# One 512 KB output store split into four pieces of 128 KB, issued over three steps of the schedule

## The reference, cut to what matters

```python
xn = _layernorm(x, axis=-1)
# attention: 16 heads of 64, rotary q and k, a distance bias kb per head
scores = jnp.einsum('bhqd,bhkd->bhqk', q, k) * SCALE
attn = jax.nn.softmax(scores + kb[None], axis=-1)
out = jnp.einsum('bhqk,bhkd->bhqd', attn, v)      # -> (8, 512, 1024) @ out_w.T -> (8, 512, 256)
# experts: 16, top 1, at most 256 tokens each; relu(x w1) w2, times the gate
x = x + attention(xn) + experts(xn)
```

## Time and profile before

| | |
|---|---|
| median of three runs | 1230.52 us |
| the profiled execution's own time | 1232.55 us |
| its span, first to last instruction | 1230.8 us |
| mean granted TensorE clock | 0.944 |
| TensorE busy | 1086.2 us (88%) |
| VectorE busy | 1014.4 us (82%) |
| ScalarE busy | 999.5 us (81%) |
| GpSimd busy | 817.6 us (66%) |
| stores of line 1183 | 7, first issued at 481.6 us, last at 1136.3 us |

### The profile page before, as it was taken

One profiled execution on the slowest core, in us unless ns is written; L12 is line 12 of the kernel. 1 busy time (PEld: TensorE's weight loads), 2 busy tenths in 40 slices (PEclk: granted clock), 3 DMA queues, 4 the chain that ended last, 5 costly groups with the idle time before them and its releaser, 6 DMA issues.

```text
span 1230.8 us, 35480 instructions
## 1 busy us (share of the span) xinstructions
PE 1086.2 (88%) x14436; PEld 797.2 (65%) x14436; DVE 1014.4 (82%) x2061; ACT 999.5 (81%) x1986; POOL 817.6 (66%) x481
## 2 busy tenths in 40 slices
PE   4840699999789999999999999999999998999874
PEld 4830588989556666666666666666666666666653
DVE  7883799999578888888898788888988887888872
ACT  2694688886279898899889899889889898988991
POOL 3135100000399988888899789888998898898741
PEclk8565799999899999999999999999999999999996
DMA  8716566773136565766665666575557657756673
GB/s 252 296 40 213 180 221 224 255 243 134 35 61 126 117 102 116 148 104 93 143 129 94 123 130 109 100 143 117 105 113 148 97 109 131 129 95 114 106 123 69
DMA packets 390289, 165.79 MB, mean 135 GB/s; under 512 B 340722, under 2 KB 380671, under 8 KB 390128
## 3 DMA queue, kind: packets, MB, share of 16 engines
q1 hardware_dynamic: 377856, 143.26, 54.4%
q0 software_dynamic: 4352, 12.41, 2.9%
q10 hardware_dynamic: 7920, 7.87, 2.1%
HBM read 58.79 MB, written 21.00 MB: 65 GB/s over the span
## 4 chain that ended last, share of the span: by engine, by line
PE 38%; DMA 13%; ACT 10%; POOL 7%; issue 4%; SPq 2%; DVE 1%; POOLq 0%; ACTq 0%
DMA pt_dma<-prob_parts 9%; PE ps_s L1377 8%; PE ps_x L1333 8%; PE ps_o L1410 7%; PE ps_t L1390 6%; ACT prob L1130 6%; PE ps_x L1352 5%; PE ps_x L1343 4%; DMA ot<-ctx_parts 4%; POOL prob_parts L1005 3%; ACT pt_pe L1114 2%; POOL ctx_parts L1013 2%; SPq L949 1%; POOL parts L999 1%; ACT val_hi L1093 1%
## 5 line engine op out<-in xcount | busy, mean ns | idle before, releaser
L1130 ACT ACTIVATE prob<-prob,neg_max 128x512 f32<-128x512 f32 x512 | 364.0, 714 | 4.7 <-DVE neg_max L1251 2.6
L1251 DVE CUSTOM_DVE_ANT_0 prob<-ps_s,strips,score_scale 128x512 f32<-128x512 f32 x512 | 360.1, 745 | 7.5 <-PE ps_s L1377 5.7
L1005 POOL TENSOR_TENSOR prob_parts<-prob,prob_parts 128x1024 f16<-128x1024 f32 x128 | 273.6, 2138 | 55.4 <-ACT prob_parts L1120 55.1
L1377 PE MATMUL ps_s<-parts 32*128 32x512 f16 x3072 | 189.1, 376 | 1.1 <-DVE parts L1297 1.0
L1257 DVE SCALAR_TENSOR_TENSOR pt_pe<-ps_t,pt_pe 128x1024 f16<-128x1024 f32 x128 | 155.8, 1217 | 36.0 <-ACT pt_pe L1114 36.0
L1390 PEld LDWEIGHTS ps_t<-ident,prob 128*128 128x128 f32 x1024 | 109.7, 141 | 57.3 <-issue 39.0
L995 POOL TENSOR_TENSOR rot<-prods 128x1024 f32<-128x1024 f32 x61 | 144.3, 2366 | 2.7 <-DVE prods L1217 2.7
L1333 PE MATMUL ps_x<-xcur,wqkv_hi 128*128 128x512 f16 x480 | 143.3, 380 | 2.7 <-DVE pt_dma L1217 1.3
L1390 PE MATMUL ps_t<-ident,prob 128*128 128x128 f32 x1024 | 139.8, 279 | 3.0 <-DVE pt_pe L1257 3.0
L1120 ACT CAST prob_parts<-prob 128x1024 f16<-128x1024 f32 x128 | 133.6, 1044 | 2.1
L1114 ACT ACTIVATE pt_pe<-ps_t 128x1024 f16<-128x1024 f32 x128 | 130.7, 1021 | 3.4 <-PE ps_t L1390 3.3
(11 more groups left out here) (207 smaller groups left out, 2639.5 us busy)
## 6 DMA issues: line engine op xcount, KB each, us to landing
raw<-in_L_ffn_w_dram SPq DMA_DIRECT2D x32, 1024.0 KB, 5.2
xa<-in_L_attn_x_dram SPq DMA_DIRECT2D x8, 512.0 KB, 6.6
xt_dram<-xth SPq DMA_DIRECT2D x8, 512.0 KB, 5.1
slots_dram<-zeros SPq DMA_DIRECT2D x4, 1024.0 KB, 8.2
xa<-slots_dram SPq DMA_DIRECT2D x16, 256.0 KB, 5.3
expert_dram<-xa POOLq DMA_DIRECT2D x16, 256.0 KB, 6.7
xcur<-xt_dram SPq DMA_DIRECT2D x8, 512.0 KB, 4.5
res<-in_L_attn_x_dram ACTq DMA_DIRECT2D x8, 512.0 KB, 4.0
```

The lines of the kernel that those rows point to most:

```text
L1005: nc.gpsimd.tensor_tensor(prob_parts[:, n % 2, 1], prob[:, (2 * n + 1) % 3], prob_parts[:, n % 2, 0], ALU.subtract).then_inc(prob_lo, 1)
L1130: nc.scalar.activation(prob[:, s % 3, q, :], prob[:, s % 3, q, :], ACT.Exp, bias=neg_max[:, 2 * (s % 3) + q:2 * (s % 3) + q + 1], scale=-1 ...
L1251: nc.vector.tensor_tensor_reduce(prob[:, s % 3, q, :], ps_s[u][:], strips[:, HG * j + u, start:start + S], score_scale[:, 0:1], 3.0e38, AL ...
L1377: last = nc.tensor.matmul(ps_s[h][:], parts[rows, 2 * F % 5, a, f, t * P:(t + 1) * P], parts[rows, (2 * F + 1) % 5, c, f, :], start=(i == ...
```

## The change

The one store of 512 KB becomes four of 128 KB, one for each of the four blocks of 128 rows: the first behind quad 4, the second behind quad 5, the third and fourth together behind quad 6. Each adds 16 to `y_stored`, so the two waits on it count 64 a batch.

```diff
-            sp.wait_ge(y_stored, 16 * NB)
+            sp.wait_ge(y_stored, 64 * (NB - 1) + 16)
...
-                if q == 4 and b:
+                if 4 <= q <= 6 and b:
                     act.wait_ge(x_free, fills_before(b, 8))
-                    act.dma_start(out[b - 1].rearrange("(t p) m -> p t m", p=P), yacc[:]).then_inc(y_stored, 16)
+                    for t in ((0,), (1,), (2, 3))[q - 4]:
+                        act.dma_start(out[b - 1, t * P:(t + 1) * P, :], yacc[:, t, :]).then_inc(y_stored, 16)
...
-                    wait(dve, y_stored, 16 * b)
+                    wait(dve, y_stored, 64 * b)
```

## The result

The changed kernel takes 1247.23 us (median of 6 runs, 1239.94 to 1251.41); the kernel before, beside it, 1230.77 us (6 runs, 1230.05 to 1232.17). The ratio is 1.0128, with a 95% interval of 1.0098 to 1.0159: 1.0 to 1.6% slower, 16.5 us by the medians. The forecast was 1235.2 us, 4.7 us slower, and the range ended at 1239.5. The direction and the place were right and the size was not. The runs of the changed kernel also spread over 11.5 us, those of the kernel before over 2.

What follows compares the result with a forecast made beforehand. No single engine is full and the order of waits decides, with TensorE the bound around the change. Terms 0 + 0 + 3.2 + 1.5 = 4.7 us slower gave 1235.2 us, range 1229.8 to 1239.5.

Steps and rivals of the forecast that it cites:

- Removed: 0: End of quad 4: taking away seven 512 KB stores frees no waiting engine, 0 us; bound on a gain 3.5 us.
- The rival on the faster side: End of quad 4: the old store holds back the probability transposes, the pieces do not; 3.5 us faster, 1227.0 us; chance 0.08.
- Added to ScalarE: 0: Behind quads 5 and 6: three more issues a batch at about 0.39 us are covered by casts, 0 us.
- That rival: End of quad 6: ScalarE is held by the two issues, up to 5.5 us on top, about 1240 us; chance 0.08.
- VectorE's wait: 3.2 us: Quad 7: `read_y` waits for the last piece, delaying TensorE's fill y1 past its slack by 3.2 us in all.
- I take 1.9 + 0.6 = 2.5 after its issue, T6 + 2.9: Behind quad 6: last piece lands after the smallest DMA's 1.9 us plus 0.6 us of data, in every batch.
- T6: In each batch, the start of the cast that ends quad 6; the forecast counts issue, landing and `read_y` from it.
- the far end, T6 + 4.6: Behind quad 6: the last piece lands like the longest 512 KB store, 4.2 us; 13.4 us slower, 1244 us; chance 1 in 20.
- The slack of 0.6 us: Quad 7: `read_y` ends before y1 starts, behind 1.40 us of value products, so 0.6 us of delay is covered.
- The further 1.1 us that I gave batch 4: Quad 7, batch 4: TensorE already waits there for a transpose DMA, so 1.1 us more of delay is covered.
- Traffic: 1.5 us: Behind quad 6: pieces take DMA time from the transpose TensorE needs; 0.5 us each in batches 1, 4 and 6.
- Rival C: In the probe: a queue's packets wait for a copy in flight on the other, so pieces land in about 4.5 us.

Runs made afterwards that it cites:

- The change without its hold: The changed kernel with plain copies for transposes, but its two pieces behind quad 6 read a constant table and VectorE does not wait for them; 1219.7 us, ratio 0.9874.
- the base: The kernel before with its transposing DMAs replaced by plain copies of the same 512 KB in 256-byte packets; 1220.4 us, ratio 0.9874 to the kernel before.
- the probe: A separate kernel with only two queues, ScalarE's storing pieces and SyncE's loading or copying beside them; two pieces alone land in 2.30 to 2.34 us.
- the change with copies: The changed kernel with its transposing DMAs replaced by plain copies of the same 512 KB in 256-byte packets; 1246.3 us, ratio 1.0071 to the kernel before.

## Why the prediction was wrong

**Removed: 0.** Right as far as the runs resolve. The change without its hold has three of the four pieces out of the gap and takes the base's time, 1219.7 for 1220.4 us, so taking the store out of its gap frees nothing. The rival on the faster side falls.

**Added to ScalarE: 0.** Right, 0.84 us for both issues, and 0.96 us to the next instruction. That rival falls too.

**VectorE's wait: 3.2 us.** Right in its mechanism, wrong in its size. The step that failed is "I take 1.9 + 0.6 = 2.5 after its issue, T6 + 2.9" for all batches. It holds where no load is ahead of the pieces and the transpose is over early: batch 7 T6 + 2.5, batch 2 T6 + 2.9, and the probe has 2.3 us from the first issue. It fails a little in batches 1 and 6, T6 + 3.4 and 3.6, where the transpose moves until T6 + 2.1 and 2.3, and most where the `xcur` load is ahead: T6 + 4.3 to 5.5. Set against the same seven starts of the kernel before, `read_y` is later by 0.8, 1.0, 4.2, 3.2, 2.8, 0.8 and 1.3 us, 14.0 in all, where my holds sum to 6.8. Of these TensorE waits 9.3 us, where I had 3.2. The chance of the far end, T6 + 4.6, which I put outside the range as needing "as long as the slowest whole store", was judged by the piece's own bytes and not by what was queued before it. I had the row for it: a share of 1.03 and 1.14 in that stretch.

**The slack of 0.6 us.** Right, but for batch 4. The seven waits of TensorE ahead of y1 are 0.20, 0.24, 3.11, 2.52, 2.29, 0.23 and 0.70 us, 9.3 in all. They are 0.5 to 0.7 us less than the delay of `read_y` in six batches and 1.1 less in batch 3. The further 1.1 us that I gave batch 4, for its wait on the transpose, was not there: 3.2 us of delay, 2.5 of wait.

**Traffic: 1.5 us.** Wrong, there is no sign of it, and the sharing went the other way. TensorE's waits for `pt_dma` fell by 1.6 us. The pieces took nothing from the transpose, since none of their packets moved until it was over or, in batch 4, in its last 0.6 us, and then they shared with the load.

**Missing: the clock.** No term and no rival had it. In batch 3 y1 and the scores took 2.74 + 2.68 us for 1.31 + 1.41, 2.7 us on top of the wait, and in batch 4 2.74 + 1.58, 1.6 us. From T6 of batch 3 to T6 of batch 6 the changed kernel took 340.1 us and the kernel before 326.8. These 13.3 us are the whole difference of the spans, 13.0. The three waits in that stretch (7.9 us) and the slow matmuls behind two of them (4.3) make 12.2 of it; the rest I have not traced. By the medians the change costs 16.5 us, so 3.5 more, of which the two profiled executions say nothing.

That a fall of the clock comes from the wait ahead of it is argued from the order in time, and was not tested by itself. For it: two of three long holds here and five places of the change with copies, against none in the same kernel without the hold. But it is not peculiar to the hold. In attention the kernel before has one fall too, behind a wait for a transpose:

```profile
689.39 0.20 PE L1410 MATMUL ps_o<-val_hi,pt_dma 128*128 128x64 f16 x1 [2.58 <-DMA pt_dma<-prob_parts]
```

```profile
689.50:692.80 3.30, 3.30 (x35) 2.69 (x35) 1.91 (x3) 1.36 (x4) 1.12 (x1) 0.50 0.83 159
```

And a wait of 2.3 us in batch 5, or of 2.6 in batch 2 of the change with copies, was followed by none.

The spread of the changed kernel's runs fits an order of two queues' issues that differs from batch to batch, each difference worth 1 to 2 us of hold; this too is argued and not shown.

## What to carry to other kernels

A transfer that something waits for is priced from its issue to its reader, with everything queued ahead of it on the other queues, and not by its own bytes. Moving a store from a gap to the last quad before its reader turned 12 us of spare time into a wait. Whether two pieces or the whole store stood there made no difference (2.0% both); with one piece the loss was 0.7%. And where a wait lands on TensorE, look at the granted clock behind it before taking the wait for the whole price.

## What the runs showed of the hardware

A transposing DMA in flight on one queue held back plain packets of the other. In the changed kernel, batch 1, from T6 + 0.9 to T6 + 2.0, the issue is past and only SyncE's queue q1 moves packets (queue, packets, MB, share of 16 engines; packets' times overlap here, so that it passes 100%):

```profile
q1 hardware_dynamic: 1246, 0.32, 127.4%
```

In six of the seven batches the pieces' first packets came as the transpose's last ones ended, at T6 + 1.1 to 2.2; in batch 4 they came 0.6 us before its end, when its packets had already grown few. Beside a plain copy both queues can move. In the probe, pieces issued at 34.21 behind a copy, these are the stretches from 35.1 to 35.7 and from 36.0 to 36.6 us; the copy is in flight in both:

```profile
q1 hardware_dynamic: 509, 0.13, 95.5%
...
q10 hardware_dynamic: 124, 0.11, 57.4%
q1 hardware_dynamic: 221, 0.06, 40.9%
```

The copy too held them back at first (alone, the probe's pieces move from 0.8 us after their issue), and then both moved. So Rival C holds in part.

Beside a plain load it went both ways. In the changed kernel, batch 4, from T6 + 2.8 to T6 + 3.8, the two queues moved as many packets each, the load's of 4 KB and the pieces' of 1 KB:

```profile
q1 hardware_dynamic: 75, 0.31, 77.4%
q10 hardware_dynamic: 72, 0.07, 20.7%
```

In the change with copies, batch 3, from T6 + 1.5 to T6 + 2.9, the load's moved alone, although the pieces were issued at T6:

```profile
q1 hardware_dynamic: 88, 0.31, 80.9%
```

The Trainium skill says (page "DMA: Bandwidth & Descriptors", section "Queues, rings and completion order") that an engine goes round robin between its queues, a packet at a time. The trace agrees in batch 4, with 75 packets for 72. It does not agree beside a transpose, nor where the load's packets moved alone for 1.4 us. The same page's section "Anatomy of one DMA" gives its fixed cost for DMAs issued from GpSimd, while these stores are issued from ScalarE, which my prediction did not say. By its formula, as an estimate, a 128 KB piece takes 2.3 us and a 512 KB store 3.2. The probe has 2.3 us for two pieces and 3.0 to 3.2 for the whole store.
